# Cross-attention kernel: transfers issued in another order, output bias inside the output projection, narrower statistics and x, values spread on fewer slots

## The reference

```
q = x @ w_q;  k, v = text @ w_k, text @ w_v;  k_ip, v_ip = ip_h @ w_k_ip, ip_h @ w_v_ip
out_text = softmax(q k^T / 4) v                # over the 69 text keys
out_ip   = softmax(q k_ip^T / 4 + mask) v_ip   # over 8 image keys, mask from boxes
out = (out_text + out_ip) @ w_out + b_out + x
```

## Time and profile before

| what | value |
|---|---|
| median of 3 runs | 1266.85 us (1266.10 to 1272.72) |
| span of the profiled execution, first to last instruction | 1263.2 us |
| mean granted TensorE clock | 0.979 |
| HBM traffic | 101 GB/s over the span |
| preparation, up to the first scores | some 260 us |

### The profile page before, as it was taken

One profiled execution on the slowest core, in us unless ns is written; L12 is line 12 of the kernel. 1 busy time (PEld: TensorE's weight loads), 2 busy tenths in 40 slices (PEclk: granted clock), 3 DMA queues, 4 the chain that ended last, 5 costly groups with the idle time before them and its releaser, 6 DMA issues.

```text
span 1263.2 us, 34240 instructions
## 1 busy us (share of the span) xinstructions
PE 1158.1 (92%) x12734; PEld 1114.9 (88%) x12734; DVE 1044.3 (83%) x2054; ACT 897.6 (71%) x1923; POOL 904.7 (72%) x1004
## 2 busy tenths in 40 slices
PE   6998887559999999999999999999999999999996
PEld 5898787459999999999999999999999999999985
DVE  5687975669888889888898888888888888898972
ACT  2343343448888888877888888888888888887773
POOL 0111101038889889988988988898898899898896
PEclk9999999779999999999999999999999999999998
DMA  6388887645555545544455554454555555555431
GB/s 173 66 181 168 156 182 149 102 91 111 116 116 120 120 114 121 120 115 114 114 120 120 121 117 115 115 116 115 117 117 115 118 120 117 123 117 114 102 82 61
DMA packets 361460, 151.31 MB, mean 120 GB/s; under 512 B 298640, under 2 KB 350864, under 8 KB 360016
## 3 DMA queue, kind: packets, MB, share of 16 engines
q1 hardware_dynamic: 361296, 149.13, 52.9%
HBM read 88.17 MB, written 39.90 MB: 101 GB/s over the span
## 4 chain that ended last, share of the span: by engine, by line
PE 53%; POOL 11%; DMA 11%; SPq 9%; DVE 6%; issue 5%; ACT 2%; POOLq 0%; ACTq 0%; DVEq 0%
PE ps_a L832 9%; DMA q_hi_extra<-q_hi_lo 8%; PE ps_o L903 8%; PE ps_s L873 7%; PE ps_m L854 6%; PE ps_s L879 6%; PE ps_b L832 6%; POOL prob_lo L1402 6%; PE ps_k L199 2%; PE ps_v L199 2%; SPq L617 2%; SPq L668 2%; POOL y L1396 2%; DMA x_keep<-in_x_dram 2%; PE ps_a L918 2%
## 5 line engine op out<-in xcount | busy, mean ns | idle before, releaser
L1402 POOL TENSOR_TENSOR prob_lo<-prob,prob_hi 128x512 f16<-128x512 f32 (+1 forms) x448 | 506.1, 1148 | 106.0 <-ACT prob_hi L1071 106.0
L873 PE MATMUL ps_s<-q_hi_lo,keys 128*128 128x256 f32 x960 | 248.9, 299 | 44.3 <-DMA q_hi_extra<-q_hi_lo 42.9
L1070 ACT ACTIVATE prob<-ps_s 128x512 f32<-128x512 f32 (+1 forms) x448 | 254.2, 567 | 35.4 <-PE ps_s L879 31.0
L1071 ACT ACTIVATE prob_hi<-ps_s 128x512 f16<-128x512 f32 (+1 forms) x448 | 252.8, 564 | 0.0
L879 PE MATMUL ps_s<-q_hi_extra,keys 128*128 128x256 f32 x960 | 234.1, 281 | 0.3 <-ACT q_hi_extra L1058 0.3
L1298 DVE TENSOR_REDUCE stats<-ps_m 128x8 f32<-128x552 f32 x320 | 231.2, 722 | 0.0
L873 PEld LDWEIGHTS ps_s<-q_hi_lo,keys 128*128 128x128 f32 x960 | 172.6, 190 | 54.1 <-issue 37.4
L903 PE MATMUL ps_o<-values,prob_hi 128*128 128x68 f16 (+7 forms) x3584 | 200.9, 193 | 1.5 <-DVE heads L1312 1.5
L903 PE MATMUL ps_o<-values,prob_lo 128*128 128x68 f16 (+3 forms) x1792 | 190.8, 193 | 0.0
L903 PEld LDWEIGHTS ps_o<-values,prob_hi 128*128 128x128 f16 x3584 | 174.9, 98 | 13.0 <-issue 1.6
L879 PEld LDWEIGHTS ps_s<-q_hi_extra,keys 128*128 128x128 f32 x960 | 173.5, 190 | 0.5 <-ACT q_hi_extra L1058 0.5
(11 more groups left out here) (180 smaller groups left out, 2999.1 us busy)
## 6 DMA issues: line engine op xcount, KB each, us to landing
x_in<-in_x_dram SPq DMA_DIRECT2D x64, 320.0 KB, 3.8
q_hi_extra<-q_hi_lo SPq DMA_DIRECT2D x64, 320.0 KB, 3.4
x_keep<-in_x_dram SPq DMA_DIRECT2D x64, 320.0 KB, 3.2
out_dram<-y SPq DMA_DIRECT2D x128, 160.0 KB, 1.8
k_scratch<-k_stage SPq DMA_DIRECT2D x16, 770.0 KB, 5.8
keys<-k_scratch SPq DMA_DIRECT2D x256, 48.1 KB, 2.1
ctx_in<-in_ctx_dram SPq DMA_DIRECT2D x64, 128.0 KB, 2.8
keys<-k_scratch SPq DMA_DIRECT2D x256, 24.1 KB, 1.9
```

The source lines that it names most:

```text
L873: mm(ps, keys[:, n, 0, quad, c:c + P], q_hl[n][:, quad, :], start=i == 0, stop=False)
L1070: nc.scalar.activation(prob[:, s, 0:w], ps_s[(b[1] + s) % 2][:, 0:w], ACT.Exp)
L1071: nc.scalar.activation(prob_hi[par(b)][:, s, 0:w], ps_s[(b[1] + s) % 2][:, 0:w], ACT.Exp).then_inc(s_hi, 1)
L1402: nc.gpsimd.tensor_tensor(prob_lo[par(b)][:, s, 0:w], prob[:, s, 0:w], prob_hi[par(b)][:, s, 0:w], ALU.subtract).then_inc(s_lo, 1)
```

## The change

1. **Order of SP's transfers.** A step issues copy_q first, then the stores of batch n-3 (before n-2), the residual of n-1 (before n), the keys of n+2 (before n+3), the values of n+2, and x of n+4. The stores of the last batch follow after the loop. The transfers of the last tail values (`store_tail`), before all in steps 0 and 1, are issued one tile a step in steps 1 to 7.
2. **Output bias.** `add_bias` on POOL is gone. aT2 becomes two tiles: the first holds hi in both halves, the second ones in rows 0 and 32, zeros elsewhere in the upper half, and lo below. The third blocks of wo hold hi above lo, and the bias (hi in row 0, lo in row 32) above hi. The number of matmuls is the same. `bias_rows` writes the rows of ones in step 1, `split_out` prepares wo.
3. **Statistics** take 64 columns, from 0, and a 64-column transpose.
4. **x without doubled columns**: one load; the third transpose has 64 columns. w_q is loaded without doubled columns as well.
5. **Values** are spread in five instructions over the slots that each tile owns (3+2, 5, 4+4 slots).

```diff
+SPREADS = [[(0, 3, 5, 3), (12, 1, 1, 2)], [(1, 3, 5, 5)], [(2, 3, 1, 4), (7, 3, 1, 4)]]
...
-            aT2 = sb("aT2", [P, S], f32r, st)
+            aT2 = [sb(f"aT2_{n}", [P, S], f32r, st) for n in ("hi", "lo")]
...
-                        sp.dma_start(x_in[par(b)][:, :, 0:D], xb).then_inc(s_x[par(b)], 16)
-                        sp.dma_start(x_in[par(b)][:, :, D:DW], xb[:, :, 256:D]).then_inc(s_x[par(b)], 16)
+                        sp.dma_start(x_in[par(b)][:], xb).then_inc(s_x[par(b)], 16)
...
                     def step(sp, b, n):
-                        E, A, Bs, Cs, Ds = has(n)
-                        if A:
+                        if 0 <= n + 1 < NB:
                             copy_q(off(b, 1))
-                        if n is None or n + 4 < NB:
+                        if 0 <= n - 3 < NB:
+                            store(off(b, -3), 0)
+                            store(off(b, -3), 1)
+                        if 0 <= n - 1 < NB:
+                            load_residual(off(b, -1))
+                        if 3 <= n + 2 < NB:
+                            sp.wait_ge(s_sc, at(b, PAIRS, 0))
+                            load_keys(off(b, 2))
+                        if 2 <= n + 2 < NB:
+                            sp.wait_ge(s_vx, at(b, 3, 3))
+                            load_values(off(b, 2))
+                        if n + 4 < NB:
                             sp.wait_ge(s_xt, at(b, 1, 3))
                             load_x(off(b, 4))
-                        if Ds:
-                            store(off(b, -2), 0)
-                            store(off(b, -2), 1)
-                        if Bs:
-                            load_residual(b)
-                        if n is None or 0 <= n < NB - 2:
-                            sp.wait_ge(s_vx, at(b, 3, 3))
-                            load_values(off(b, 2))
-                        if n is None or 0 <= n < NB - 3:
-                            sp.wait_ge(s_sc, at(b, PAIRS, PAIRS))
-                            load_keys(off(b, 3))
-                        if n in (0, 1):
-                            for u in range(4 * n, min(4 * n + 4, len(TILES_IN))):
-                                store_tail(1, u)
+                        if 0 <= n - 1 < len(TILES_IN):
+                            store_tail(1, n - 1)
...
-                            last = nc.tensor.transpose(ps_b[:, c:c + P], x_in[par(b)][:, t, 256:DW], ident[:])
+                            last = nc.tensor.transpose(ps_b[0:DL, c:c + P], x_in[par(b)][:, t, 256:D], ident[:])
...
-                        terms += [(both, w[n][:, 2, cols]) for n in range(2)]
+                        terms += [(third_hi, w[0][:, 2, cols]), (third_lo, w[1][:, 2, cols])]
...
-                            last = nc.tensor.transpose(ps_m[:, 0, t * P:(t + 1) * P], stats[:, t, :], ident[:])
+                            last = nc.tensor.transpose(ps_m[0:NSTAT, 0, t * P:(t + 1) * P], stats[:, t, :], ident[:])
...
-                            nc.scalar.activation(aT2[0:64, :], ps_b[0:64, 0:S], ACT.Copy, scale=f[0:64]).then_inc(s_ahi, 1)
+                            nc.scalar.activation(aT2[0][:], ps_b[:, 0:S], ACT.Copy, scale=f).then_inc(s_ahi, 1)
...
+                    def split_out(raw):
+
+                        then(nc.vector.tensor_copy(wo[0][:, 0:2, :], raw[:, 0:2, :]))
+                        nc.vector.tensor_tensor(wo[1][:, 0:2, :], raw[:, 0:2, :], wo[0][:, 0:2, :].bitcast(fp32), ALU.subtract)
+                        nc.vector.tensor_copy(wo[0][0:64, 2, :], raw[0:64, 2, :])
+                        then(nc.vector.tensor_copy(wo[1][64:P, 2, :], raw[64:P, 2, :]))
+                        then(nc.vector.tensor_tensor(wo[0][64:P, 2, :], raw[64:P, 2, :], wo[1][64:P, 2, :].bitcast(fp32), ALU.subtract))
+                        nc.vector.memset(wo[1][0:64, 2, :].bitcast(fp32), 0.0)
+                        then(nc.vector.tensor_copy(bias_hl[0].bitcast(f32r), bias[:]))
+                        then(nc.vector.tensor_tensor(bias_hl[1], bias[:], bias_hl[0], ALU.subtract))
+                        nc.vector.tensor_copy(wo[1][0:1, 2, :], bias_hl[0][0:1, :])
+                        then(nc.vector.tensor_copy(wo[1][32:33, 2, :], bias_hl[1][32:33, :]))
...
+                        def bias_rows():
+                            for q in range(4):
+                                dve.wait_ge(s_vst[q], 32 * (2 * NI // 4))
+                            nc.vector.memset(aT2[1][0:64, :].bitcast(fp32), 0.0).then_inc(s_z, 1)
+                            dve.wait_ge(s_z, 3)
+                            for r in (0, 32):
+                                nc.vector.memset(aT2[1][r:r + 1, :].bitcast(fp32), 1.0).then_inc(s_z, 1)
...
-                            t = slice(GTILE[g], GTILE[g] + GTILES[g])
-                            nc.vector.tensor_tensor(
-                                v[:, t, :, 2:SLOT],
-                                raw_v[par(b)][:].rearrange("p t (o c) -> p t o c", o=1)[:, t]
-                                .broadcast_to([P, GTILES[g], SLOTS, 2 * DH]),
-                                own_rows[:].rearrange("p t (n c) -> p t n c", n=SLOTS)[:, t], ALU.mult).then_inc(s_vx, 1)
+                            for t, count, stride, slots in SPREADS[g]:
+                                tt = slice(t, t + (count - 1) * stride + 1, stride)
+                                last = nc.vector.tensor_tensor(
+                                    v[:, tt, 0:slots, 2:SLOT],
+                                    raw_v[par(b)][:].rearrange("p t (o c) -> p t o c", o=1)[:, tt].broadcast_to([P, count, slots, 2 * DH]),
+                                    own[:, tt, 0:slots, :], ALU.mult)
+                            last.then_inc(s_vx, 1)
...
+                        if n == 1:
+                            bias_rows()
...
-                                pool.wait_ge(s_xb, at(d, 1, 1))
+                                pool.wait_ge(s_xk[par(d)], nth(d, 16))
...
-                        if Cs:
-                            add_bias()
```

More of the change, by code:

```diff
@@ L41 @@
 REG = KOFF + 3 * P
-R_MT, R_MI, R_MASK, R_ONE = 64, 64 + H, 64 + 2 * H, 64 + 2 * H + NIP
+R_MT, R_MI, R_MASK, R_ONE = 0, H, 2 * H, 2 * H + NIP
+NSTAT = 64
 KC = 4
 DW = D + 64
+DL = D - 2 * P
 HT = 64
@@ L88 @@
 VCOLS = TILES * SLOTS * SLOT
+SPREADS = [[(0, 3, 5, 3), (12, 1, 1, 2)], [(1, 3, 5, 5)], [(2, 3, 1, 4), (7, 3, 1, 4)]]
+assert all(NSLOTS[t + n * d] == slots for group in SPREADS for t, count, d, slots in group for n in range(count))
 def bank_tiles(half):
@@ L111, in constants @@
             col = sel[:, h // 4, KOFF + (h % 4) * KEYS + k]
-            col[(R_MT if k < T else R_MI) + h] = -1.0
+            col[QD + (R_MT if k < T else R_MI) + h] = -1.0
             if k >= T:
-                col[R_MASK + k - T] = 1.0
-            col[R_ONE] = 1.0
+                col[QD + R_MASK + k - T] = 1.0
+            col[QD + R_ONE] = 1.0
     ones = np.zeros((P, VCOLS), np.float32)
@@ L161, in xattn_kernel @@
         own_rows = sb("own_rows", [P, TILES, SLOTS * (SLOT - 2)], fp16)
-        wq = [sb(f"wq_{n}", [P, 3, 384], f32r) for n in ("hi", "lo")]
+        wq = [sb(f"wq_{n}", [P, 3, D], f32r) for n in ("hi", "lo")]
         wo = [sb(f"wo_{n}", [P, 3, D], f32r) for n in ("hi", "lo")]
         mask = sb("mask", [P, NT, NB * NIP], fp32)
-        bias = sb("bias", [P, D], fp32)
         values = [sb(f"values{q}", [P, VCOLS], fp16) for q in range(2)]
@@ L442, in xattn_kernel @@
             with ExitStack() as st:
-                raw_q = sb("raw_q", [P, 3, 384], fp32, st)
+                raw_q = sb("raw_q", [P, 3, D], fp32, st)
                 raw_o = sb("raw_o", [P, 3, D], fp32, st)
                 raw_c = sb("raw_c", [P, VCOLS], fp32, st)
+                bias = sb("bias", [64, D], fp32, st)
+                bias_hl = [raw_q[0:64, n, :] for n in range(2)]
                 box = sb("box", [P, NB, 4, 4], fp32, st)
@@ L515, in xattn_kernel @@
             heads = [sb(f"heads{n}", [P, 2 * H, DH], fp32, st) for n in range(2)]
-            x_in = [sb(f"x_in{q}", [P, NT, DW], fp32, st) for q in range(2)]
+            x_in = [sb(f"x_in{q}", [P, NT, D], fp32, st) for q in range(2)]
             xT = [sb(f"xT_{n}", [P, 2, S], f32r, st) for n in ("hi", "lo")]
@@ L640, in load_main @@
                                          bbox.rearrange("b m c -> (b m c)").partition_broadcast(P)).then_inc(s_w2, 16)
-                            sp.dma_start(bias[:], b_out.partition_broadcast(P)).then_inc(s_w2, 16)
+                            sp.dma_start(bias[:], b_out.partition_broadcast(64)).then_inc(s_w2, 16)
                         if n == 3:
@@ L926, in project_out @@
                         ps = (ps_a, ps_b)[t]
-                        split_product(ps[:, 0:D], lambda k: aT[0][:, k, c], lambda k: aT[1][:, k, c], aT2[:, c],
+                        split_product(ps[:, 0:D], lambda k: aT[0][:, k, c], lambda k: aT[1][:, k, c], aT2[0][:, c], aT2[1][:, c],
                                       wo, slice(0, D), False,
```

(9 more changed lines are left out.)

24 lines of the change are left out of this document (12 added, 12 removed).

## The result

The changed kernel is slower: 1286.75 us in the median of 4 runs (1284.6 to 1288.7). Its ratio to the kernel before is 1.015, with a 95% interval of 1.013 to 1.017. The profiled execution spans 1282.8 us, 19.6 more than before. The once-a-step matmul splits them, counted from the one a step before the first of the earlier trace rows (at 276.79 us before, 272.72 after): 4.1 us less until that one, 26.7 us more over the 61 steps behind it, 3.0 us less from the last one to the end.

A forecast was written before the change was run, and what follows sets the result against it. PE was taken as the bound, held up by a late copy of q; -39.1 (steady) + 0.3 (head) - 4.8 (tail) = -43.6 us took the span from 1263.2 to 1219.6, the median to 1223.3, range 1208 to 1242.

The forecast's parts named there:

- the spread of values: On DVE: five instructions take 1.7 to 2.1 us a step against 2.39, off the path, counted as nothing.
- Rival (b): Steady steps: another engine's lag shows once PE never stops; steps of 14.95 us add 14 us, giving 1238; chance 0.12.
- The stops for the copy of q: Steady steps: issuing the copy first on SP ends PE's waits, 15.36 to 14.71 us a step, -39.1 us.
- my sum: Whole span: -39.1 + 0.3 - 4.8 = -43.6 us, from 1263.2 to 1219.6.
- forecast +0.3: Head of the kernel: SP loads, DVE's weight preparation and memsets sum to +0.3 us, from -2 to +3.
- forecast 4.8: Tail: POOL without its bias addition saves 2.0 us in two steps and 2.8 us in step 64.
- PE's floor: Steady steps: without stops each costs PE's own 14.71 us, and DVE, POOL and ACT keep up.
- The bias: POOL's add_bias, 1656 ns a step, goes; counted as nothing in the steady part because POOL had slack.
- Narrow transposes: PE's transposes of x and the statistics with 64 stationary columns: taken as 0, at the other end -13.6 us.
- rival (a): PE: narrow transposes pay, spacing falls from 0.11 to about 0.06 us, time by 13.6 to 1209.7; chance 0.12.
- Rival (c): SP: the reorder does nothing and the copy of q goes out at the old distance; some 1262 us; chance 0.04.
- rival (d): SP: keys, loaded one step ahead behind stores and residual, come late; steps of 15.7 us, 1288 us; chance 0.06.

The follow-up runs named there:

- e6: Changed kernel with POOL's subtraction for prob_lo replaced by a memset to 0: 1216.9 us, ratio 0.960 to the kernel before.
- e12: Kernel of e11 with its extra DVE instruction moved behind the first normalization of heads, where POOL idles: 1220.6 us, ratio 0.964 to the kernel before.
- e7: e1 plus two small DVE instructions a step, each reading two SBUF tiles, behind the first and second spread: 1291.4 us, ratio 1.020 to the kernel before.
- e11: e1 plus one extra DVE instruction reading two 64-column SBUF tiles, behind the first spread: 1291.2 us, ratio 1.020 to the kernel before.
- e8: e1 plus two small DVE instructions a step, each reading one SBUF tile, behind the first and second spread: 1219.8 us, ratio 0.963 to the kernel before.
- e1: Changed kernel with only the spread of values put back to three instructions over 5 slots: 1220.7 us, ratio 0.965 to the kernel before.
- e9: e1 with a tile of zeros added to x_keep on POOL where add_bias stood: 1247.0 us, ratio 0.985 to the kernel before.
- e3: Kernel before with only the new order of SP's transfers: 1250.1 us, ratio 0.988 to the kernel before.
- e10: e1 with the old order of SP's transfers: 1257.9 us, ratio 0.993 to the kernel before.
- e4: Changed kernel with all 2080 columns of values spread by one instruction: 1255.1 us, ratio 0.992 to the kernel before.

## Why the prediction was wrong

**The step that failed** is the spread of values: "the new ones take 1.7 to 2.1", by nanoseconds a column, and "DVE gets 0.3 to 0.7 us a step". They took 4.32 in the steady part. Two errors lie in it. First, 969 ns for 800 columns beside 449 for 480 is no rate: 320 more columns cannot cost more than the first 480. That was the mark of a wait inside the duration, and I turned it into a price a column. The dense instructions need 0.58 and 0.41 us undisturbed in the first steps of the kernel before (timeline of DVE):

```profile
267.97 0.58 DVE L1333 TENSOR_TENSOR values<-raw_v,own_rows 128x800 f16<-128x800 f16 x1
...
270.69 0.41 DVE L1333 TENSOR_TENSOR values<-raw_v,own_rows 128x480 f16<-128x480 f16 x1
```

So they need 1.57 us a step, and 0.82 of the 2.39 was waiting. The five new ones need 0.31 + 0.18 + 0.40 + 2 x 0.35 = 1.6 us of their own (e6, e12), no less than the three: the columns saved were eaten by the two further starts. What grew was waiting, from 0.8 to 2.7 us a step. Before, the three start with some 0.5, 0.45 and 0.2 us left of the POOL instruction under way; after, four of the five start with 0.6, 0.8, 1.1 and 0.9 us left (means in the timelines, 400 to 1200 us). There is one collision more, and each comes earlier in POOL's instruction.

The Trainium skill states the rule ("SBUF — State Buffer", section "Who interferes with whom"): a VectorE instruction with two SBUF inputs and a GpSimd instruction that reads SBUF cannot run together; the later one is blocked until the other has finished. The runs agree with it: beside a POOL instruction that reads, 64 columns take 0.86 us with two SBUF inputs (e7, e11) and 0.21 with one (e8), and 0.18 where POOL idles (e12). By that rule each further instruction can bring a further wait, so the five could come out dearer; I had not weighed it.

Second, that DVE "is not on the path" had a margin of 1.1 us in a step of 14.7. One instruction's 0.9 us should have just fitted, and e11 shows that it does not: beside its own 0.86 us the third spread grows by 0.81 and the second by 0.39, 2.1 us of DVE's time in all, and the step by 1.2. Once DVE is late, PE's scores, then ACT's exponentials, then POOL's prob_lo follow it, so POOL idles 0.5 to 1.0 us ahead of most prob_lo, and DVE's next spread comes just behind the start of one: 0.05 and 0.25 us in the rows of the changed kernel above, 0.13 us for the third spread of e11 (timelines of DVE and of POOL), where e1 has it 0.20 us before the end of one.

```profile
708.54 1.30 DVE L1356 TENSOR_TENSOR values<-raw_v,own_rows 128x480 f16<-128x480 f16 x1
```

```profile
708.41 1.17 POOL L1431 TENSOR_TENSOR prob_lo<-prob,prob_hi 128x512 f16<-128x512 f32 x1 [0.99 <-ACT prob_hi L1073]
```

That the lateness feeds on itself is shown by the third spread of e11; that the chain over PE and ACT carries it is read from timelines, not tried by itself. No run delayed DVE by as much without a collision either, so what of the 1.2 us is lateness and what the further collisions is not told apart. Rival (b) had the right kind of mechanism, another engine's lag, at a fifth of its size.

**Point by point, the rest.** The stops for the copy of q: right, in cause and price. In the changed kernel the copy went out 0.7 us after the last projection matmul started (714.16 in SP's timeline, 713.45 in PE's), and from 400 to 1200 us no stop was left. e1, which is the change without the new spread, has a span of 1217.4 us against the 1219.6 of my sum. Its 61 steps take 40.9 us less (39.8 by the forecast's rate), the time to the first 1.5 less (forecast +0.3), the end 3.4 less (forecast 4.8). PE's floor was called at 14.71 us and is 14.68.

The bias was mis-sized: 0 in the steady part, where e9 finds 26 us. In the old order POOL had slack; in the new one the residual comes later, and the addition would have been on the path. Both parts are needed: the order alone brings 16 us (e3), the rest of e1 without it 9 (e10), both 45 (e1), each against the kernel before measured beside it.

Narrow transposes: next to 0, as taken; rival (a) is out. For x the weight load fell from 140 to 111 ns and the matmul stayed at 272 ns, as the groups by form show, the first line before, the others after:

```profile
L819 PEld LDWEIGHTS ps_b<-ident,x_in 128*128 128x128 f32 x104 | 14.6, 140 | 0.0
```

```profile
L820 PE MATMUL ps_b<-ident,x_in 128*64 128x128 f32 x102 | 27.8, 272 | 0.0
...
L820 PEld LDWEIGHTS ps_b<-ident,x_in 128*64 128x64 f32 x102 | 11.3, 111 | 0.0
```

In e1, too, the start of such a transpose lies 0.11 us behind the start of the one ahead and 0.07 us before the next, as it did before. The transposes of the statistics gained a little, 0.086 us to the next start before and 0.072 in e1, twice a step; that is as much as PE's floor fell, 0.03 us.

Rival (c), an order that does nothing, and rival (d), keys that come too late, did not occur: PE waited neither for the copy nor for keys in e1. In the tail POOL's part went as said, a little less of it.

The best version tried is e1: the change with its spread left as it was, 3.5% faster than the kernel before and 5% faster than the change.

## What to carry to other kernels

Count DVE instructions that read two SBUF tiles beside a POOL that reads SBUF, not their columns: each waits for what is left of POOL's instruction, up to the whole of it, so few long ones can beat many short ones, and the place decides (here 0.18 or 0.86 us). But one very long one can cost more in latency than it saves (e4). When durations of two sizes fit no line through a positive start, look for a wait inside them before using them as a rate, and take the own time from a stretch where the other engine idles.

## What the runs showed of the hardware that I had not expected

A lone instruction of 64 columns added 70 us to 1221 (e11), through 0.86 us a step of its own and 1.2 that it caused in the second and third spread. The collision goes both ways: POOL's three prob_lo took 3.92 us in e1 where two take 2.29 undisturbed, and its y addition 1.87 us in e4 where it takes 0.87. What a DVE instruction pays can be read off: of some 2200 with two SBUF inputs that start during a POOL instruction that reads SBUF, all runs together, all but 26 end a fixed time after it, within 0.01 us, among them 0.05 us for 64 columns, 0.17 for 288, 0.22 for 384, 0.27 for 480 and 0.43 for 800, each some 0.13 to 0.15 us less than the instruction takes alone. A memset on POOL held up neither of the two sizes that met one, 288 and 384 columns (e6). The weight load of an fp32 transpose shrank by 29 ns for half the columns; that of the projections is 53 ns shorter at half the columns. The matmuls of x's transposes and of the projections take the same time at either width.
